# Earlier gathers and later splits on GpSimd, four gather places, and id tables behind the LoRA operands

## What is computed

```python
x = x + L0_ffn(L0_cond(x, weights, cond_id), lora_A, lora_B, W, bias, lora_weights)
Bx = einsum('bni,bri->bnr', x, B[adapter_id])            # rank 16
h  = einsum('bnr,bor->bno', Bx, A[adapter_id])
Wg, Wu, Wd = dequant(gate...), dequant(up...), dequant(down...)   # NF4[codes] * scale, 2752 hidden
x = x + (silu(h @ Wg.T) * (h @ Wu.T)) @ Wd.T
```

## Time and profile before

| | us |
|---|---|
| three runs | 1142.51, 1137.14, 1139.64 |
| median | 1139.64 |
| profiled execution, its own time | 1142.35 |
| its span, first to last instruction | 1140.7 |
| its mean granted clock of TensorE, of 1 | 0.928 |

### The profile page before, as it was taken

One profiled execution on the slowest core, in us unless ns is written; L12 is line 12 of the kernel. 1 busy time (PEld: TensorE's weight loads), 2 busy tenths in 40 slices (PEclk: granted clock), 3 DMA queues, 4 the chain that ended last, 5 costly groups with the idle time before them and its releaser, 6 DMA issues.

```text
span 1140.7 us, 16184 instructions
## 1 busy us (share of the span) xinstructions
PE 1016.9 (89%) x5586; PEld 870.8 (76%) x5586; DVE 901.1 (79%) x1346; ACT 787.5 (69%) x993; POOL 331.8 (29%) x337
## 2 busy tenths in 40 slices
PE   6999999999996899787789778887898988789998
PEld 5888888888885788676678667766777867668887
DVE  4999989889998599786788668886796987765354
ACT  4888879789796599675678557775667966664321
POOL 4021121211203244334331343333323422433220
PEclk8999999999998799898898888997888988989999
DMA  9765365383443488575556556656566846468896
GB/s 254 195 154 129 96 164 125 91 201 97 104 106 75 110 187 192 120 171 120 120 115 144 120 128 132 131 113 143 124 144 132 173 93 137 108 153 185 197 322 242
DMA packets 95264, 166.77 MB, mean 146 GB/s; under 512 B 10416, under 2 KB 63424, under 8 KB 95184
## 3 DMA queue, kind: packets, MB, share of 16 engines
q0 software_dynamic: 24416, 86.02, 36.7%
q1 hardware_dynamic: 69440, 78.66, 24.5%
q10 hardware_dynamic: 1328, 1.05, 0.3%
HBM read 101.22 MB, written 72.88 MB: 153 GB/s over the span
## 4 chain that ended last, share of the span: by engine, by line
PE 67%; DMA 9%; DVE 8%; POOL 6%; ACT 5%; issue 5%; POOLq 0%; DVEq 0%; ACTq 0%
PE ps_y L1271 15%; PE ps_z L1271 14%; PE ps_z L1107 14%; DMA gath<-table,row_at 8%; PE ps_gu L1246 7%; POOL st_hi L574 4%; PE ps_gu L1174 3%; PE ps_t L1162 3%; ACT ring L667 3%; DVE val L863 3%; PE ps_t L1174 2%; PE ps_y L1094 2%; PE ps_gu L1125 2%; DVE val L865 1%; PE ps_t L1117 1%
## 5 line engine op out<-in xcount | busy, mean ns | idle before, releaser
L667 ACT ACTIVATE ring<-codes 128x1024 f32<-128x1024 int32 x455 | 456.7, 1053 | 2.8 <-DVE val L863 1.6
L863 DVE TENSOR_TENSOR val<-val,ring 128x512 f32<-128x512 f32 x520 | 327.1, 691 | 25.2 <-ACT ring L667 24.8
L865 DVE SCALAR_TENSOR_TENSOR val<-ring,val 128x512 f32<-128x512 f32 x390 | 246.8, 690 | 7.3 <-ACT ring L667 6.9
L1246 PE MATMUL ps_gu<-bx_p,gath 96*128 96x128 f32 x704 | 106.9, 299 | 109.4 <-DMA gath<-table,row_at 109.4
L1246 PEld LDWEIGHTS ps_gu<-bx_p,gath 96*128 96x128 f32 x704 | 105.5, 218 | 124.4 <-DMA gath<-table,row_at 104.9
L574 POOL TENSOR_TENSOR st_hi<-ga_f,one 128x128 fp32r<-128x128 f32 x42 | 65.1, 1550 | 375.4 <-ACT ga_f L707 355.5
L799 ACT ACTIVATE inter<-ps_gu 128x512 f32<-128x512 f32 (+1 forms) x96 | 53.9, 561 | 173.6 <-PE ps_gu L1246 172.9
L1025 DVE TENSOR_TENSOR inter<-ps_gu,inter 128x512 f32<-128x512 f32 (+1 forms) x96 | 61.8, 644 | 130.8 <-PE ps_gu L1246 92.3
L637 POOL DMA_DIRECT2D out<-staged x80 | 76.7, 959 | 219.5 <-ACT staged L812 219.5
L603 POOL DMA_INDIRECT gath<-table,row_at x96 | 111.8, 1164 | 63.7 <-PE ps_gu L1246 40.9
L1107 PE MATMUL ps_z<-we_hi,y_hi 128*128 128x512 f32 x256 | 105.6, 413 | 0.2 <-DVE y_lo L924 0.2
(11 more groups left out here) (152 smaller groups left out, 1779.5 us busy)
## 6 DMA issues: line engine op xcount, KB each, us to landing
out<-staged POOLq DMA_DIRECT2D x80, 512.0 KB, 6.5
codes<-in_L_ffn_down_codes SPq DMA_DIRECT2D x21, 512.0 KB, 4.1
xs<-in_x SPq DMA_DIRECT2D x16, 512.0 KB, 3.9
out<-in_L_ffn_bias SPq DMA_DIRECT2D x4, 2048.0 KB, 14.3
out<-xs POOLq DMA_DIRECT2D x16, 512.0 KB, 5.9
ring<-out SPq DMA_DIRECT2D x16, 512.0 KB, 5.7
out<-ring SPq DMA_DIRECT2D x15, 512.0 KB, 3.6
codes<-in_L_ffn_gate_codes SPq DMA_DIRECT2D x12, 512.0 KB, 4.5
```

Source lines behind the costliest of these rows:

```text
L667: act.activation(ring[:, (k - 1) % RING, :], codes[:, n % 2, :], ACT.Identity, bias=offset, scale=slope).then_inc(lines, 1)
L863: ins = dve.tensor_tensor(into, into, line, pick)
L865: ins = dve.scalar_tensor_tensor(out=into, in0=line, scalar=add, in1=into, op0=ALU.add, op1=pick)
L1246: ins = pe.matmul(ps[:, k * P:(k + 1) * P], gath[0:KP, w % GS, (2 * k + m) * P:(2 * k + m + 1) * P], bx_p[0:KP, t * P:(t + 1) * P], start= ...
```

## The change

- GS, the places of gath and of their semaphores, goes from 3 to 4, and FETCH from 4 to 5, so that a slot issues the gather of work s+4, which waits until gate_up of work s is done. INR goes from 3 to 2: in_hi of a work now waits for the down products of two slots before.
- In a slot GpSimd's order is now fetch, accumulate, split.
- The first four gathers are issued in the last four tiles of the first phase, one in each.
- VectorE makes the LoRA operands first and selections() behind them.
- Two setup buffers change places in memory.

```diff
-    INR = 3
-    GS = 3
+    INR = 2
+    GS = 4
     AHEAD = 2
-    FETCH = 4
+    FETCH = 5
...
+        ad_braw = sb("ad_braw", [P, D], F32, setup)
         la = sb("la", [P, D], F32, setup)
-        ad_braw = sb("ad_braw", [P, D], F32, setup)
...
                 if 1 <= t <= NT - CR:
                     load_conds(t + CR - 1)
+                if t >= NT - GS:
+                    fetch(t - NT + GS)
             store_x1(NT - 1)
-            for w in range(GS):
-                fetch(w)
...
             for slot in range(WORKS):
-                if is_gu(TURN_AT.get(slot - 1)):
-                    split_ga(TURN_AT[slot - 1])
-                if GS <= slot + FETCH - 1 < WORKS:
+                if slot + FETCH - 1 < WORKS:
                     fetch(slot + FETCH - 1)
                 if 0 < slot <= LAST:
                     accumulate(slot - 1)
+                if is_gu(TURN_AT.get(slot - 1)):
+                    split_ga(TURN_AT[slot - 1])
...
-            selections()
             dve.wait_ge(lora_b_in, 16 * 2)
...
                               ).then_inc(lora_lo_ready, 1)
+            selections()
             at = 0
```

## The result

The changed kernel takes 998.51 us (median of 4 runs, 998.48 to 1000.38) against 1138.39 of the kernel before beside it (4 runs, 1126.64 to 1142.51): a ratio of 0.879, interval 0.8724 to 0.8856. The forecast was 1007, the range 993 to 1050.

A forecast was written before the change was run, and what follows sets the result against it. Late gathers behind GpSimd's splits were taken to keep half the run waiting, with VectorE the next bound. Gains 117 + 12.5 + 3 = 132.5 off 1142.35 give 1009.9, about 1007 us at the median; range 993 to 1050.

The forecast's parts named there:

- The bound and the order: Slots, 449.6 to 1033.5 us: gathers behind splits come late; the new order removes all 19 waits, VectorE sets the pace.
- The room: Slots: about 18 us from a split's product to the gather's use, for a chain of 14 us, 20 at longest.
- The share of VectorE: Slots, 449.6 to 1033.5 us: VectorE's 457.23 us of work fill 98% of 466.6 us; gain 117 us, best end 124.
- The nearest row: 883 to 919 us, same loop without a late gather: VectorE busy 35.90 of 36.00 us, a guide to its share.
- The share of TensorE: Slots: TensorE's busy time falls from 488.33 to about 420 us as the clock's lower level goes.
- Two places of in_hi: Slots: in_hi must wait for slot s-1's down products, not s-2's; nothing taken beyond the 98%.
- rival two: Slots: the in_hi wait bites and 39 us come back as VectorE's idle time, 1046 us; chance 0.09.
- The first gathers: End of the first phase: first products start 10.8 us earlier, some 3 us more from the clock; 12.5 us taken.
- The id tables: Start: LoRA operands begin 4 us earlier with the tables behind them; ends 0 and 4, 3 us taken.
- Rival three: Slots: a split gets through only when VectorE is idle, so the kernel gets slower, 1168 us; chance 0.03.
- Rival one: Slots: VectorE holds GpSimd off, gathers stay late though less; 65 us lost, 1072 us; chance 0.15.
- Rival four: Slots: gathers still held up by the accumulate now ahead; a few us, within the forecast's range; no separate chance.

The follow-up runs named there:

- x8_inr3: The changed kernel with three places for in_hi and in_lo again, paid for by three places for the condition matrices instead of four: 997.81 us.
- x4_first_late: The changed kernel with the first four gathers behind the last x1 store again: 1008.2 us, 9.7 us more than the changed kernel.
- x5_ids_first: The changed kernel with the id tables first on VectorE again: 1001.75 us, 3.2 us more than the changed kernel.
- x9_four_on_pe: The changed kernel with four late up units turned by TensorE and put down by ScalarE, in place of VectorE: 998.64 us, ratio 0.8764.

## Why the prediction was right, and where not

**The bound and the order: right.** The measured 998.51 us lies in the range, at the best end of the forecast (998). All 19 waits of the earlier trace rows are gone, VectorE sets the pace, and the granted clock is 1.00. That the gathers did it is shown by the three kernels with one slot less: part of the waits comes back, and the stretch is 11 to 16 us longer.

**The room: too wide, and partly luck.** The prediction took 18 us for the room and 14 us, or 20 with the longest of each, for what has to fit. The room is 15.3 us in the median. The sum of the chain counted the gather's issue twice, since the landing of the earlier trace rows is measured from the start of the issue, and left out the second half of the split, which took 0.5 to 5.7 us in the changed kernel's stretch. The errors partly cancel; the longest chain was 15.1 us. That no wait at all is left is right by 0.2 us.

**The share of VectorE: too careful.** The term was 117 us, from 98% of 457.23 us, and its best end 124. It is 130.0. VectorE is busy 452.83 of 453.90 us, 99.8%: with 457.23 us of work, that share instead of 98% makes the stretch 8 us shorter. The other 4.4 us are that the busy time itself fell from 457.23 to 452.83. The instructions are as many, 654, and hardly shorter one by one (the times of all of them add up to 504.9 us before and 504.2 after); rows that follow each other at once overlap by about 0.1 us, and rows behind a wait do not. So idle time taken away gives back a little more than itself. The nearest row, 35.90 of 36.00, was the better measure.

**The share of TensorE: mis-sized, at no cost here.** The prediction let TensorE's 488.33 us fall to about 420, by taking the whole time at the lower clock level, some 140 us, as work. It is 441.57 at clock 1.00. In the kernel before the lower level held for 136.5 us of the stretch, and TensorE was busy in 99.9 of them; the rest was the waiting itself. Half of 99.9 off 488.33 leaves 438. So VectorE leads TensorE by 11 us and not by 37, which is why taking work from VectorE soon meets TensorE.

**Two places of in_hi: right.** Three places change nothing (x8_inr3), and rival two did not come. ScalarE does wait for the down products, but at the end, where TensorE sets the pace.

**The first gathers: 12.5 forecast, 10.3 gained.** The start moved as said: 0.6 us behind bx_p. The doubtful part was the clock, and it did not come back. After a pause of only 2.64 us the products ran at the lower level (six matmuls 1.41 us), and the granted clock from 361.5 to 369 was 0.54, as it was 0.50 from 375.2 to 384 before. A small wait is new: ScalarE's evacuation at 371.47 waits 1.98 us for an x1 store to land. x4_first_late puts the whole part at 9.7 us.

**The id tables: right, the size only roughly.** 3 forecast, 2.9 in the traces, 3.2 by x5_ids_first. But the first W product starts at 39.3 to 42.5 us in the eleven traces with the new start and at 43.0 to 43.2 in the three with the old one, so single traces put the gain anywhere from 0.5 to 3.9 us; the means differ by 2.2.

**Rival three: false.** GpSimd gets through with VectorE at work. The longest split of the changed kernel, in order of time:

```profile
493.24 6.92 POOL L574 TENSOR_TENSOR st_hi<-ga_f,one 128x128 fp32r<-128x128 f32 x1 [4.29 <-ACT ga_f L707]
500.24 0.47 POOL L576 TENSOR_TENSOR st_lo<-ga_f,st_hi 128x128 fp32r<-128x128 f32 x1
```

and VectorE beside it:

```profile
492.66 0.68 DVE L1025 TENSOR_TENSOR inter<-ps_gu,inter 128x512 f32<-128x512 f32 x1
493.26 1.22 DVE L893 TENSOR_TENSOR val<-val,d_scales 128x1024 f32<-128x1024 f32 x1
494.39 2.49 DVE L865 SCALAR_TENSOR_TENSOR val<-ring,val 128x512 f32<-128x512 f32 x4
496.80 0.68 DVE L1032 TENSOR_TENSOR in_lo<-inter,in_hi 128x512 fp32r<-128x512 f32 x1
497.40 1.29 DVE L865 SCALAR_TENSOR_TENSOR val<-ring,val 128x512 f32<-128x512 f32 x2
498.61 1.29 DVE L863 TENSOR_TENSOR val<-val,ring 128x512 f32<-128x512 f32 x2
499.81 0.68 DVE L1025 TENSOR_TENSOR inter<-ps_gu,inter 128x512 f32<-128x512 f32 x1
```

It stood through ten VectorE instructions that follow each other at once, all with two inputs in SBUF, and ended 0.35 us after the product began, whose one input is in PSUM. The Trainium skill, "SBUF — State Buffer", section "Who interferes with whom", lets the second instruction wait for the first to finish; here it waited through ten. The same section of the Trainium skill infers that descriptor generation is not held by such instructions; a gather's issue was held for 7.59 us in x9_four_on_pe.

A product is not the only opening. Another split of the changed kernel got through between two instructions that both have two inputs in SBUF:

```profile
544.32 2.77 POOL L574 TENSOR_TENSOR st_hi<-ga_f,one 128x128 fp32r<-128x128 f32 x1 [4.30 <-ACT ga_f L707]
...
544.34 2.49 DVE L863 TENSOR_TENSOR val<-val,ring 128x512 f32<-128x512 f32 x4
...
546.86 1.31 DVE L893 TENSOR_TENSOR val<-val,d_scales 128x1024 f32<-128x1024 f32 x1
```

The scale (L893) here follows the merge that it needs, and starts 0.03 us after that one's end, where rows that follow each other at once overlap. At 493.26 it did overlap, and the split stayed held. Of the 22 GpSimd instructions in the changed kernel's stretch that took over 2 us (splits and gathers' issues), 13 ended 0.2 to 0.9 us after the start of an instruction that reads PSUM, 8 beside such a pause of 0.03 to 0.04 us before a scale, and one beside VectorE's transposition (L873). None of the 22 let such an opening pass while it was held. A held instruction costs up to one slot, at most 7.6 us in these traces.

**Rival one: right in its mechanism, and closer than its 0.15 tells.** The sum had one slot lost to the split and a gather of 0.97 us. The experiments show that the gather's issue is held for a whole slot too (7.59 us), which the 4.07 of the earlier trace rows did not reach. With both, 18.3 us are needed, 3 more than the room measured. In the changed kernel the two never fall together, and nothing in the change sees to that: with four VectorE instructions moved elsewhere they do twice, and cost TensorE some 6 us. That they did not fall together is luck.

**Rival four: did not come.** No gather's wait is left, and the accumulates ahead of the gathers took 0.93 to 1.01 us each.

## What to carry to other kernels

Before you shorten a stage, work out for its late input the room from the point where it can start to the point of its use, from rows of the trace rather than in whole steps of the loop, and hold the longest chain against it, not the median; a step more of room takes a queue's stalls away without making any of them shorter. Where VectorE runs without a pause, count a GpSimd instruction that reads SBUF, or an issue of a gather, as a whole period between two points where VectorE lets it through (here mostly the products that read PSUM; for splits also a pause of 0.03 us before an instruction that needs the one before it), and count that for each of them in a row. And a small edit that should take work from the bound engine, and gains nothing, may have moved such an instruction past its opening: look for the returned wait before you call another engine the bound.

## What was not expected of the hardware

- GpSimd's issue of an indirect gather, 0.97 us when undisturbed, takes up to 7.6 us beside VectorE instructions with two inputs in SBUF, and the landing then comes 10.8 to 12.6 us after its start, where the median in the kernel before was 6.4. The accumulates on the same queue are never held (0.93 to 1.01 us each of the 63 in the stretch). A gather reads its row numbers (row_at) from SBUF and an accumulate's issue has no such list; that this is the reason is argued, not shown.
- Behind a pause of 2.64 us TensorE ran at the lower clock level (granted clock 0.54 over the next 7.5 us), much as behind one of 13.40 us (0.50 over 8.8).
- VectorE's busy time for the same count of instructions is 4.4 us less in the stretch when nothing makes it wait; 0.6 of them are shorter instructions, the rest is that rows that follow each other at once overlap.
